# An edge softmax whose maximum is found in two steps, and a first group of output rows made by VectorE, in a two-layer graph network

## What is computed

```python
h = x @ W
s1 = h @ a1
s2 = h @ a2
e = leaky_relu(s1[src] + s2[dst], negative_slope=0.2)
attention = softmax(e)                      # over all 25,000 edges
output = segment_sum(attention[:, None] * h[src], dst, num_segments=50000)
x = layernorm(x + output)
```

## Time and profile before

| What | Value |
|---|---|
| median of 3 runs | 1059.08 us (1057.36 to 1061.64) |
| profiled execution | 1056.71 us |
| its span | 1055.0 us |
| busy share of the span: PE, DVE, ACT, POOL | 63%, 77%, 67%, 72% |
| mean DMA rate over the span | 187 GB/s |

### The profile page before, as it was taken

One profiled execution on the slowest core, in us unless ns is written; L12 is line 12 of the kernel. 1 busy time (PEld: TensorE's weight loads), 2 busy tenths in 40 slices (PEclk: granted clock), 3 DMA queues, 4 the chain that ended last, 5 costly groups with the idle time before them and its releaser, 6 DMA issues.

```text
span 1055.0 us, 14618 instructions
## 1 busy us (share of the span) xinstructions
PE 662.7 (63%) x3270; PEld 448.6 (43%) x3270; DVE 807.1 (77%) x3723; ACT 705.4 (67%) x2036; POOL 761.1 (72%) x801
## 2 busy tenths in 40 slices
PE   0467777777787677787655656656566555556640
PEld 0246555555565555565444545545432111111110
DVE  4789999999988798896876666666548777777760
ACT  3659998999899797997423444534447666666650
POOL 6777777777777777777077777777737777777775
PEclk9979998999889898988868787878858788778775
DMA  7666786787767678657348777887743322332310
GB/s 200 197 190 200 222 278 210 237 264 231 226 220 238 213 222 258 202 194 226 122 140 285 254 255 248 277 271 248 222 132 93 96 85 86 88 94 85 88 43 25
DMA packets 82013, 196.90 MB, mean 187 GB/s; under 512 B 19814, under 2 KB 22005, under 8 KB 81916
## 3 DMA queue, kind: packets, MB, share of 16 engines
q1 hardware_dynamic: 56774, 148.35, 43.3%
q0 software_dynamic: 25152, 47.63, 16.0%
HBM read 122.71 MB, written 77.22 MB: 190 GB/s over the span
## 4 chain that ended last, share of the span: by engine, by line
POOL 42%; issue 19%; DVE 15%; DMA 8%; ACT 8%; PE 7%; DVEq 1%; SPq 0%; POOLq 0%; ACTq 0%
POOL xs L484 24%; POOL h_res L484 16%; ACT xsT L888 5%; DMA xs<-x_all,row_tab 4%; DVE nst L1408 4%; DVE node_out L1390 4%; POOL out_dram L488 2%; DMA h_res<-in_x,dst_tab 2%; DVE match L1041 1%; DVE part L1395 1%; DVE nmv L1416 1%; ACT logs L898 1%; PE psum L674 1%; PE psum L680 1%; PE psum L597 1%
## 5 line engine op out<-in xcount | busy, mean ns | idle before, releaser
L484 POOL DMA_INDIRECT xs<-x_all,row_tab x196 | 187.7, 958 | 86.9 <-issue 83.0
L488 POOL DMA_INDIRECT out_dram<-yb,at_last x196 | 195.1, 995 | 76.1 <-issue 54.2
L484 POOL DMA_INDIRECT xs<-in_x,src_tab x196 | 187.0, 954 | 61.7 <-issue 58.8
L484 POOL DMA_INDIRECT h_res<-in_x,dst_tab x196 | 187.3, 956 | 59.7 <-issue 59.7
L725 ACT ACTIVATE h_res<-node_in,shift,rstd 128x128 f32<-128x128 f32 (+1 forms) x392 | 155.7, 484 | 0.3 <-DVE shift L1168 0.3
L700 PE MATMUL psum<-node_out,ident_inv 128*128 128x512 f32 x98 | 73.1, 836 | 97.5 <-DVE node_out L1390 97.5
L866 ACT ACTIVATE xsT<-psum 128x512 f32<-128x512 f32 x48 | 28.7, 597 | 145.5 <-PE psum L680 145.2
L1390 DVE SCALAR_TENSOR_TENSOR node_out<-node_out,same_prev,xsT 128x128 f32<-128x128 f32 x196 | 68.6, 350 | 48.5 <-ACT xsT L888 36.2
L725 ACT ACTIVATE yb<-psum,shift,rstd 128x128 f32<-128x128 f32 x196 | 73.6, 455 | 29.2 <-DVE shift L1401 26.5
L552 PE MATMUL psum<-h_res 128*128 128x512 f32 x98 | 59.3, 690 | 41.9 <-ACT h_res L732 41.8
L680 PE MATMUL psum<-ident,xs 128*128 128x128 f32 x192 | 39.8, 344 | 72.7 <-DMA xs<-x_all,row_tab 72.6
(11 more groups left out here) (279 smaller groups left out, 1806.9 us busy)
## 6 DMA issues: line engine op xcount, KB each, us to landing
x1d_in<-x_all SPq DMA_DIRECT2D x98, 256.0 KB, 3.9
node_in<-in_x SPq DMA_DIRECT2D x48, 512.0 KB, 4.3
x_all<-h_res SPq DMA_DIRECT2D x48, 512.0 KB
out_dram<-node_out SPq DMA_DIRECT2D x48, 512.0 KB, 3.3
x_all<-yb SPq DMA_DIRECT2D x49, 256.0 KB, 2.6
src_b<-src_t SPq DMA_DIRECT2D x49, 256.0 KB, 7.3
node_in<-x_all SPq DMA_DIRECT2D x24, 512.0 KB, 5.8
h_res<-in_edge_attr SPq DMA_DIRECT2D x7, 784.0 KB
```

The source lines that it names most:

```text
L484: return pool.indirect_dma_start(out=to, out_offset=None, in_=table, in_offset=bass.IndirectOffsetOnAxis(ap=idx, axis=0))
L488: return pool.indirect_dma_start(out=table, out_offset=bass.IndirectOffsetOnAxis(ap=idx, axis=0), in_=rows, in_offset=None, bounds_check=l ...
```

## The change

The constant `BASE` (46) divides the groups. The logits and the partition's maximum of groups 0 to 45 are taken as soon as `h_kept` is at 46; ScalarE weighs those edges by that first maximum, and group 0 is weighed and summed before group 48 is looked at. Groups 46 to 48 get the partition's full maximum. The factor between the two, `fold_p`, joins them: in the sum of all exponentials (`sum_wide`), in `scale_lead` (groups 0 to 45) against `part_scale` (groups 46 to 48), so that TensorE uses `ident_inv` for the first and `ident_last` for the others, in `same_prev` where group 46 begins, and once in `part`.

Group 0 does not go through TensorE: VectorE multiplies its sums by `scale_lead` and adds the node rows itself, in two halves of two tiles, each half with moments, shift and normed rows of its own; the node rows and results lie in SBUF. Therefore `e_y` counts from group 1, `kept(0)` stands behind both halves, and in the head loop `kept` runs for the group before.

ScalarE scales both halves of the last late chunk in step 46, so its store leaves SyncE's queue earlier, and with it the loads behind it. In the last stage `weigh` moves behind the normed rows of a group. `xa` and `agg` now lie in `src_b`, which the gather stage has done with. Some semaphore counts that nobody waited for are dropped. The diff, cut to its core:

```diff
+    BASE = GROUPS - 3
...
+        xa, agg = src_b[:, 0:2, :], src_b[:, 2:4, :]
...
+        exp_lead, exp_tail, fold_p, fall_fold, scale_lead = (scales[:, i:i + 1] for i in range(5))
         part = sb("part", [P, D])
         last_xT = match[:, :, :].rearrange("p t w -> p (t w)")[:, 0:GW]
...
+        ident_last = diag
...
-                wait(sp, e_y, g - XI + 1)
+                if g == XI:
+                    sp.wait_ge(first_y, 2)
+                wait(sp, e_y, g - XI)
                 load_x1d(sp, g, x1d_back)
...
-            pe.wait_ge(min_col, 1)
+            pe.wait_ge(min_col, 2)
...
-            for g in range(GROUPS):
+            for g in range(1, GROUPS):
                 b = bank[g % 4]
                 pe.wait_ge(x1d_back[g % XI], use(g, XI) * 16)
                 mm(b, ident[:, :], x1d_in[:, g % XI, :], start=True, stop=False)
                 pe.wait_ge(r_chain, (g + 1) * G)
-                mm(b, ident_inv[:, :], agg[:, g % 2, :], start=False, stop=True).then_inc(e_y, 1)
+                mm(b, ident_inv[:, :] if g < BASE else ident_last[:, :], agg[:, g % 2, :], start=False, stop=True).then_inc(e_y, 1)
...
-            mm(bank[4][:, 0:P], tile(agg[:, END % 2, :], G - 1), ident_inv[:, :], start=True, stop=True).then_inc(f_pe, 1)
+            mm(bank[4][:, 0:P], tile(agg[:, END % 2, :], G - 1), ident_last[:, :], start=True, stop=True).then_inc(f_pe, 1)
...
+            def weigh(g):
+                wait(act, r_chain, (g - 1) * G)
+                for t in range(G):
+                    i = g * G + t
+                    fn(tile(xa[:, g % 2, :], t), h_res[:, i * DH:i * DH + D], ACT.Copy, scale=att[:, i:i + 1])\
+                        .then_inc(xa_done, 1)
...
                 j = s // 2
-                if j < len(LATE):
-                    if j >= NO:
-                        act.wait_ge(late_stored[j % NO], use(j - NO, NO) * 16)
-                    scale_rows(node_out[:, j % NO, :], node_in[:, j % NI, :], P, HALVES[s % 2], ratio[:, LATE[j], :], None)\
-                        .then_inc(late_applied, 1)
-
-            act.wait_ge(min_col, 1)
-            fn(att[:, 0:TILES], logit[:, 0:TILES], ACT.Exp, bias=min_p[:, :], scale=-1.0, accum_out=exp_sum[:, :])\
-                .then_inc(exp_done, 1)
-            act.wait_ge(exp_done, 1)
-
-            def weigh(g, tiles=range(G)):
-                for t in tiles:
-                    i = g * G + t
-                    fn(tile(xa[:, g % 2, :], t), h_res[:, i * DH:i * DH + D], ACT.Copy, scale=att[:, i:i + 1])\
-                        .then_inc(xa_done, 1)
-
-            weigh(0, range(0, 2))
+                for half in (0, 1) if s == BASE else (s % 2,):
+                    if j < len(LATE) and s <= BASE:
+                        if j >= NO:
+                            act.wait_ge(late_stored[j % NO], use(j - NO, NO) * 16)
+                        scale_rows(node_out[:, j % NO, :], node_in[:, j % NI, :], P, HALVES[half], ratio[:, LATE[j], :], None)\
+                            .then_inc(late_applied, 1)
+                if s == BASE + 1:
+                    act.wait_ge(min_col, 1)
+                    fn(att[:, lead], logit[:, lead], ACT.Exp, bias=lead_min, scale=-1.0, accum_out=exp_lead[:, :])\
+                        .then_inc(exp_done, 1)
+                    act.wait_ge(exp_done, 1)
+                    weigh(0)
+            weigh(1)
+            act.wait_ge(min_col, 2)
+            fn(att[:, tail], logit[:, tail], ACT.Exp, bias=min_p[:, :], scale=-1.0, accum_out=exp_tail[:, :])
+            fn(fold_p[:, :], lead_min, ACT.Exp, bias=min_p[:, :], scale=-1.0).then_inc(exp_done, 1)
             act.wait_ge(min_b, 1)
             fn(fall_p[:, :], bank[3][:, 0:1], ACT.Exp, bias=max_p[:, :]).then_inc(fall_done_p, 1)
-            weigh(0, range(2, G))
-            weigh(1)
-            for s in range(GROUPS):
+            weigh(2)
+            halves = range(0, G // 2), range(G // 2, G)
+            act.wait_ge(first_var, 1)
+            fn(logs[:, 0:G // 2], nmv[:, 0, 0:G // 2, 1], ACT.Ln, bias=eps_cols[:, 0:1]).then_inc(first_log, 1)
+            act.wait_ge(first_log, 1)
+            fn(rstd[:, 0, 0:G // 2], logs[:, 0:G // 2], ACT.Exp, scale=-0.5).then_inc(first_rstd, 1)
+            act.wait_ge(first_shift, 1)
+            for t in halves[0]:
+                scale_rows(yb[:, 0, :], yb[:, 0, :], P, range(t, t + 1), rstd[:, 0, :], shift[:, 0, :])\
+                    .then_inc(first_applied, 1)
+            act.wait_ge(e_var, 1)
+            fn(logs[:, G // 2:G], nmv[:, 0, G // 2:G, 1], ACT.Ln, bias=eps_cols[:, 0:1]).then_inc(e_log, 1)
+            act.wait_ge(e_log, 1)
+            fn(rstd[:, 0, G // 2:G], logs[:, G // 2:G], ACT.Exp, scale=-0.5).then_inc(e_rstd, 1)
+            act.wait_ge(e_shift, 1)
+            scale_rows(yb[:, 0, :], yb[:, 0, :], P, range(G // 2, G // 2 + 1), rstd[:, 0, :], shift[:, 0, :])\
+                .then_inc(first_applied, 1)
+            scale_rows(yb[:, 0, :], yb[:, 0, :], P, range(G - 1, G), rstd[:, 0, :], shift[:, 0, :]).then_inc(e_applied, 1)
+            weigh(3)
+            for s in range(1, GROUPS):
                 act.wait_ge(e_var, s + 1)
                 fn(logs[:, 0:G], nmv[:, s % 2, :, 1], ACT.Ln, bias=eps_cols[:, 0:1]).then_inc(e_log, 1)
                 act.wait_ge(e_log, s + 1)
                 fn(rstd[:, s % 2, 0:G], logs[:, 0:G], ACT.Exp, scale=-0.5).then_inc(e_rstd, 1)
-                if s > 0 and edge(s + 2):
-                    weigh(s + 2)
                 act.wait_ge(e_shift, s + 1)
                 if s >= YB:
                     act.wait_ge(e_scat[s % YB], use(s - YB, YB) * 16 * G)
-                if s == 0:
-                    for t in range(G - 1):
-                        scale_rows(yb[:, 0, :], bank[0], P, range(t, t + 1), rstd[:, 0, :], shift[:, 0, :])\
-                            .then_inc(first_applied, 1)
-                scale_rows(yb[:, s % YB, :], bank[s % 4], P, range(G - 1 if s == 0 else 0, G), rstd[:, s % 2, :],
-                           shift[:, s % 2, :]).then_inc(e_applied, 1)
-                if s == 0:
-                    weigh(2)
+                scale_rows(yb[:, s % YB, :], bank[s % 4], P, range(G), rstd[:, s % 2, :], shift[:, s % 2, :])\
+                    .then_inc(e_applied, 1)
+                if edge(s + 3):
+                    weigh(s + 3)
...
-            lead = slice(0, END * G)
-            dve.wait_ge(h_kept, END)
-            c.link(logits(lead, logit[:, TILES:TILES + 1]))
-            dve.wait_ge(late_stored[0], use(max(j for j in range(len(LATE)) if j % NO == 0), NO) * 16)
-            v.memset(agg[:, 1, (G - 1) * D:G * D], 0.0).then_inc(agg_zero, 1)
+            def running(g, t):
+                dve.wait_ge(xa_done, g * G + (t if g == 0 else G - 1) + 1)
...
+            def kept(g, t):
+                if g == BASE and t == 0:
+                    dve.wait_ge(own_chain, g * G)
+                    c.link(v.tensor_scalar(part[:, :], part[:, :], fold_p[:, :], None, ALU.mult))
...
+            def sums_free(s):
+                if s > 1:
+                    wait(dve, e_y, s - 2)
+                    dve.wait_ge(own_chain, (s - 1) * G)
+
+            def first_rows(tiles):
+
+                for t in tiles:
+                    last = v.scalar_tensor_tensor(tile(yb[:, 0, :], t), tile(agg[:, 0, :], t), scale_lead[:, :],
+                                                  tile(x1d_in[:, 0, :], t), ALU.mult, ALU.add)
+                last.then_inc(first_y, 1)
+
+            def first_moments(tiles, done):
+                for t in tiles:
+                    last = v.bn_stats(nst[:, t, :], tile(yb[:, 0, :], t))
+                c.link(last)
+                for t in tiles:
+                    last = v.bn_aggr(nmv[:, 0, t, :], nst[:, t, :])
+                last.then_inc(done, 1)
+
+            def first_shifts(tiles):
+                return v.scalar_tensor_tensor(shift[:, 0, tiles.start:tiles.stop], nmv[:, 0, tiles.start:tiles.stop, 0], -1.0,
+                                              rstd[:, 0, tiles.start:tiles.stop], ALU.mult, ALU.mult)
+
+
+            v.memset(agg[:, 1, (G - 1) * D:G * D], 0.0)
+            dve.wait_ge(h_kept, BASE)
+            logits(lead, lead_min).then_inc(min_col, 1)
+            for t in range(G):
+                running(0, t)
...
-            logits(slice(lead.stop, TILES), min_p[:, :]).then_inc(min_col, 1)
-            dve.wait_ge(min_col, 1)
-            v.tensor_scalar(max_p[:, :], min_p[:, :], -1.0, None, ALU.mult).then_inc(max_kept, 1)
+            dve.wait_ge(h_kept, END)
+            logits(tail, min_p[:, :]).then_inc(min_col, 1)
+            dve.wait_ge(min_col, 2)
+            v.tensor_scalar(max_p[:, :], min_p[:, :], -1.0, None, ALU.mult)
+            running(1, 0)
             dve.wait_ge(min_T, 1)
             v.tensor_reduce(min_all[:, :], bank[2][0:1, 0:P], AX, ALU.min).then_inc(min_one, 1)
-            dve.wait_ge(exp_done, 1)
```

(51 more changed lines are left out.)

89 lines of the change are left out of this document (43 added, 46 removed).

## The result

The changed kernel took 1054.45 us as the median of 21 runs (1051.62 to 1058.62), the kernel before 1058.61 us in 21 runs beside it (1052.08 to 1061.64). The ratio of the two samples is 0.9968 with a 95% interval of 0.9954 to 0.9982: 3.4 us less, 1.9 to 4.9 (the two medians alone differ by 4.2). The forecast was 1056.6, 2.45 us less than the median shown, in a range of 1053.3 to 1060.6. The direction and the range were right, and the change is under the 0.5% that was called a difference.

What follows compares the result with a forecast made beforehand. GpSimd's scatter rate, 5.2 us per group, sets the pace after group 1. The first scatter's 3.8 us gain less 1.3 lost at group 1 gave 2.45: 1059.08 - 2.45 = 1056.6 us, range 1053.3 to 1060.6.

Steps and rivals of the forecast that it cites:

- Early logits: VectorE after its last lookups: logits of 46 groups start without group 47's copy, `min_p` at 779.78, gain 1.2 us.
- Group 0 without TensorE: VectorE sums group 0 itself; together with the early logits, first scatter at 786.7, 3.8 us earlier.
- The new wait at group 1: Group 1 ready at 794.0, group 0's scatters through at 791.9: a 2.1 us wait takes back 1.3 of 3.8.
- The queue of SyncE: Earlier store and four loads around the last gather: possible delay of that gather, costed at nothing.
- the bounds 0 and 1.4 us: Price of the last gather's delay by SyncE's queue: at least nothing, at most 1.4 us from a 6.6 us wait.
- From there on everything moves as one piece: Groups after 1: no further waits; group 2 ready at 798.25, due at 799.2, VectorE needing 4.25 us per group against 5.2.
- signs that the prediction itself named: Mechanism wrong if group 48's product waits for DMA, TensorE delays moments in groups 1 and 2, or waits exceed 0.3 us behind group 2.
- by then: Behind the head loop: extra fold of `part` and four `kept`, 2 us on VectorE, covered by its lead of 5.2 - 4.25 per group.
- the lower clock: Rival: TensorE at 1.2 GHz through the head groups, moments wait 0.7 us per group, gain 1 to 2 us; chance 0.10.

Runs made afterwards that it cites:

- Group 0 through TensorE: Changed kernel with group 0 sent through TensorE again, early exponential and early running sums kept; ratio to the kernel before 0.9994.
- the version with products first: Changed kernel with HEAD = 16 and, on VectorE, products of group 48 right behind the lead logits, group 0's running sums after `min_p`; ratio 0.9958.
- the second sample: The changed kernel again, unedited, timed and profiled against the kernel before; ratio 0.9986.
- HEAD = 16: Constant `HEAD` raised from 8 to 16, moving the change of loop to group 16; ratio 0.9960 on the changed kernel, 1.0010 on the kernel before.
- the version with another order on VectorE: Changed kernel with HEAD = 16, six filler matmuls, and group 1's moments, aggregates and shift ahead of `kept` of group 0; ratio 0.9971.

## Why the prediction was right, and where not

*Early logits.* Right. `min_p` came at 6.2 us after the last gather (6.6 in the second profile), foreseen 6.1. The sum gave this part 1.2 us, 1.0 with the delay in the reduction. Group 0 through TensorE has it alone and brings the first scatter 0.8 to 1.0 us ahead of the kernel before. Undoing it within the changed kernel moves the stretch by 3.86 us, because there the lead logits, with the running sums of group 0 and `min_p` behind them, start 3.6 us later (3.81 us after the last gather against 0.23); that is another comparison than the 1.2.

*Group 0 without TensorE.* First scatter foreseen 3.8 us earlier with both parts, measured 4.15 and 3.5 in the two pairs of profiles. The multiply-adds were over-priced: two took 0.61 us, not 0.8. Unlike the runnings, neither waits for the other's result, which is the likely reason; it was not tried by itself.

*The new wait at group 1.* Right in kind: 1.74 us where about 2.1 + 0.3 was foreseen. Group 1 gained 3.47 and 2.8 us instead of 2.45; its moments began at 14.9 us instead of 15.9, for the same cheaper operations and smaller differences of the same sort.

*The queue of SyncE.* Costed at nothing, rightly: no product waited for DMA in the changed kernel, and in the version with products first the gather landed at 3.7 us, 1.3 us ahead of the changed kernel's need. Of the bounds 0 and 1.4 us the lower was the true one. What the earlier store and loads do by themselves was not tried.

*"From there on everything moves as one piece."* This step failed, by signs that the prediction itself named: a wait over 0.3 us appeared behind group 2, and the idle time before group 2's moments names TensorE. I had one period of VectorE, 4.25 us, from two groups at TensorE's higher level, and named the extra `kept` behind the head loop as covered "by then". The runs show in its place periods of 5.06 and 5.19 us up to groups 2 and 3, and then 8.5 us across the change of loop. By 4.25 each, the shift of group 8 would have come 29.8 us after group 1's (786.26), at 816.0; it came at 824.73, 8.7 us later. About 4.5 us of that are longer steps before the change of loop, in which the moments of groups 2, 3, 6 and 7 wait for TensorE (0.74, 0.74, 2.19 and 0.32 us), and 4.2 are the step across it. The lead that the groups had by then covered all but 2.2 us, which is the price. The long step could have been read before: it is the 7.9 us between the shifts of groups 7 and 8 in the trace of the kernel before. I had the lower clock as a rival at 0.10 with the right mechanism (0.7 us per group, deciding only with further work on TensorE at groups 3 and 5) but not the place where it is paid.

So the hinge gave a little more than foreseen, 2.8 to 3.5 us instead of 2.45, and 2.2 of it went back at group 8, which was foreseen at nothing. By the profiles the stretch gained only 0.6 to 0.9 us; the last scatter came at 271.6 and 271.8 us after the last gather where the prediction had 270.0. The timed runs say 3.4 (1.9 to 4.9) and in the second sample 1.5 (-0.5 to 3.6). That the timed gain lies so near the forecast is therefore luck: the steps of the prediction, with the wait that it missed, account for under 1 us of it.

Whether the rest is real stays open. Over the eleven samples of the changed kernel and its variants, the timed gain is on average about 1 us more than the stretch explains (ratio times 1057.9 against the stretch less 272.5, for each row of the table), from 2.5 more to 0.3 less; for the two of the kernel before it is not. But each ratio is uncertain by 1.4 to 2 us either way, and samples that share a comparison share its error. Something ahead of the last gather, such as the dropped semaphore counts, may give that 1 us; no run tried it, and the profiles, whose last gather starts anywhere between 769.4 and 776.7, can't show it.

## What to carry to other kernels

Where an engine that works at a fixed pace follows a gap, as GpSimd with its scatters does here, a gain at the gap counts only up to the first later group that is not ready for it: work out readiness against due time for each group up to the point where the lead is safe, and above all where the order of a loop changes. Put such a change of order where the lead is large; here that was one constant and 2 us by the profile. Measure a small gain by the distance between two events on either side of the edit when the rest of the program varies by more than the gain, and start at an event of the engine on whose work the path depends: from GpSimd's last gather the first scatter varied by 0.7 us over the seven profiles with the same order up to there, from VectorE's lead logits by 0.04.

## What the runs showed of the hardware

TensorE's clock at the hinge differed between kernels and also between profiles. In both profiles of the changed kernel PEclk was 0.50 until 25 us after the last gather. In two profiles of the kernel before it was 0.96 or more from 15 to 25 us after it, behind 5 us in which TensorE was busy for 4.8 to 5.0; in the third, with HEAD = 16, it was 0.64 to 0.68 from 10 to 25 us. With group 0's matmuls back on TensorE it was 0.83 from 10 to 15 us after the last gather, and 0.66 in the profile of that version with HEAD = 16. That the missing matmuls of group 0 keep the clock low is therefore likely, but not strict: in the profile of HEAD = 16 it rose to 0.71 and 0.63 without them, and the moments waited all the same. Six small matmuls whose result nobody reads brought it to 0.87; in the version with another order on VectorE the same six did not hold it (0.63, 0.71, then 0.50 in windows of 5 us).

The distance from the last gather to the last scatter, 272 us, repeated within 0.3 us between two profiles of one kernel, while the start of the last gather moved by 2.5 and 4.3 us between them and by 7 us over all fourteen profiles. Where nothing held GpSimd up, the 192 steps from group 1's first scatter to the last took 249.6 to 250.6 us, 1.30 us each.
